# Selective scans: VectorE's C rows from SBUF through 128-fold DMA, and a fourth decay buffer

## The reference

```python
x_dbl = einsum('bld,ed->ble', x_conv, x_proj_w)      # splits into dt_in, B, C
delta = softplus(einsum('blr,dr->bld', dt_in, dt_proj_w) + dt_proj_b)
dA = exp(delta[:, :, None] * A)                      # the decay
h  = h * dA + (delta * u)[:, :, None] * B[:, None, :] # the scan over the tokens
y  = einsum('bdn,bn->bd', h, C)                      # sum over the states
```

## Time and profile before

| what | us |
|---|---|
| three runs: median (lowest to highest) | 3246.61 (3240.67 to 3251.88) |
| the profiled execution | 3240.62 |
| its span | 3238.9 |
| the stage's loop, first to last scan and product | 776.5 |
| busy over the span: TensorE / VectorE / ScalarE / GpSimd | 2954.5 / 2151.4 / 1625.0 / 1076.9 |

### The profile page before, as it was taken

How to read it: one execution, slowest core, us unless ns; L and a number is a source line. 1 busy time by engine, 2 the same in 40 slices (tenths; PEclk the granted TensorE clock), 3 DMA queues, 4 the chain that set the end, 5 groups by cost and what they waited for, 6 DMA issues and landing times. The chain is left out here.

```text
span 3238.9 us, 58361 instructions
## 1 busy us (share of the span) xinstructions
PE 2954.5 (91%) x22601; PEld 1697.9 (52%) x22601; DVE 2151.4 (66%) x4823; ACT 1625.0 (50%) x3321; POOL 1076.9 (33%) x504
## 2 busy tenths in 40 slices
PE   7888899999899999998977998898889889988998
PEld 3333344444799999743434544444454344564547
DVE  6776634545777777666568887777871559936991
ACT  3545542432433333426266776776753657725762
POOL 1111100000300000000078877777850209922990
PEclk8999999999655555699988999999899999999999
DMA  5343332022000000030442222222310101250224
GB/s 156 94 111 90 89 108 84 8 78 80 16 4 4 4 4 4 2 107 1 143 142 88 77 94 86 80 82 73 98 41 41 61 1 68 99 198 0 91 98 188
DMA packets 113492, 234.32 MB, mean 72 GB/s; under 512 B 13760, under 2 KB 50752, under 8 KB 104768
## 3 DMA queue, kind: packets, MB, share of 16 engines
q1 hardware_dynamic: 113216, 230.59, 21.9%
HBM read 185.71 MB, written 44.83 MB: 71 GB/s over the span
## 5 line engine op out<-in xcount | busy, mean ns | idle before, releaser
L2547 DVE TENSOR_TENSOR_SCAN s_hh<-psum,s_dbu 128x512 f32<-128x512 f32 x384 | 447.6, 1208 | 77.3 <-ACT psum L2159 76.1
L1272 PE MATMUL psum<-h_ring,h_parts 128*128 128x4 f16 x12264 | 478.0, 168 | 3.8 <-DVE h_ring L1414 3.5
L2417 POOL TENSOR_TENSOR s_dbu<-s_du,s_bb 128x1024 f32<-128x1024 f32 x191 | 446.7, 2360 | 67.1 <-DVE s_hh L2547 56.0
L1272 PEld LDWEIGHTS psum<-h_ring,h_parts 128*128 128x128 f16 x12264 | 429.8, 106 | 51.9 <-DVE h_ring L1414 4.2
L1334 ACT ACTIVATE h_now<-psum 128x16 f32<-128x16 f32 x1024 | 187.3, 183 | 326.8 <-PE psum L1272 322.3
L2159 ACT ACTIVATE psum<-s_delta,s_decay 128x512 f32<-128x512 f32 x384 | 256.6, 686 | 109.1 <-DVE s_hh L2547 107.0
L2051 PEld LDWEIGHTS psum<-w_c,s_term 128*128 128x128 f32 x1536 | 202.3, 151 | 136.7 <-issue 117.5
L911 DVE TENSOR_TENSOR f_hid<-f_gate,psum 128x512 f32<-128x512 f32 x184 | 126.5, 687 | 205.2 <-PE psum L837 198.2
L902 POOL MEMSET r_weights<- 128x512 f32 x4 | 2.1, 524 | 777.1 <-POOLq L1224 507.3
L1414 DVE TENSOR_SCALAR h_ring<-h_now 128x16 f16<-128x16 f32 x1024 | 183.8, 179 | 115.0 <-ACT h_now L1334 11.7
L898 ACT ACTIVATE f_gate<-psum 128x512 f32<-128x512 f32 x184 | 109.6, 597 | 281.9 <-PE psum L833 281.8
(11 more groups left out here) (543 smaller groups left out, 6047.5 us busy)
## 6 DMA issues: line engine op xcount, KB each, us to landing
s_bb<-s_wide SPq DMA_DIRECT2D x192, 256.0 KB, 3.5
x_spill<-x_flip SPq DMA_DIRECT2D x28, 1024.0 KB, 3.8
f_share<-f_wide SPq DMA_DIRECT2D x208, 128.0 KB, 3.0
s_cc<-s_wide SPq DMA_DIRECT2D x60, 256.0 KB, 3.4
a_ks<-a_spread SPq DMA_DIRECT2D x96, 128.0 KB, 3.3
a_qs<-a_spread SPq DMA_DIRECT2D x96, 128.0 KB, 3.9
x_spare<-x_spill SPq DMA_DIRECT2D x4, 2048.0 KB, 7.7
x_raw<-x_spill SPq DMA_DIRECT2D x4, 2048.0 KB, 7.5
```

The source lines that it names most:

```text
L1272: mm = nc.tensor.matmul(here[:, cols], parts[:, part, GROUP * grp + p, :], ring[:, (i - 1) % RING, grp, cut, cols], start=False, stop=True ...
L2417: nc.gpsimd.tensor_tensor(dbu[:, s % D_RING], du[:, t % 2], both(bb[:, s % B_RING, :]), ALU.mult).then_inc(dbu_ready, 1)
L2547: nc.vector.tensor_tensor_scan(hh[:, s % 4, half, :], DECAYS[i % 3], dbu[:, s % D_RING, half, :], 0.0, ALU.mult, ALU.add).then_inc(scan_do ...
```

## The change

VectorE's C products no longer read from PSUM. SP fetches the C row of every step to all partitions: `cc` gets a ring of 6, indexed by s, and the C row of step s is issued behind the B row of step s + 4. Each waits for the product with C of six steps before, whichever engine made it. With that `pick_c`, its table, GpSimd's cast, the bf16 parts, the small matmuls and four of ScalarE's five copies a turn go. Bank 3 now only carries the second half of the rates. The decay ring gets a fourth buffer in SBUF (`fourth`), so that instruction i waits for scan i - 4, and every fourth scan reads its decay from SBUF.

```diff
-    DECAYS = (bank[1], bank[4], bank[5])
+    DECAYS = (bank[1], bank[4], bank[5], fourth[:, :])
-    B_RING, C_RING = 6, 3
+    B_RING, C_RING, C_LATER = 6, 6, 4
+    DECAY_RING = 4
...
         def c_there(eng, s):
-            eng.wait_ge(c_in[pool_steps(s) % C_RING], 16 * (pool_steps(s) // C_RING + 1))
+            eng.wait_ge(c_in[s % C_RING], 16 * (s // C_RING + 1))
+        def c_used(eng, s):
+            if by_vector(s):
+                eng.wait_ge(term_vector, vector_steps(s) + 1)
+            else:
+                eng.wait_ge(term_pool, pool_steps(s) + 1)
...
                     open_pre(("rate", t))
-                    pe.wait_ge(dt_kept, t + 1)
+                    parts_there(pe, t)
-                    pe.wait_ge(term_vector, vector_steps(s))
-                    nc.tensor.matmul(PICK_C, w[f"dtw{r}"][:, P:2 * P], dt[0:rank, :], start=True, stop=True).then_inc(rate_ready, 1)
+                    pe.wait_ge(delta_done, t)
+                    nc.tensor.matmul(RATE, w[f"dtw{r}"][:, P:2 * P], small[0:rank, :], start=True, stop=True).then_inc(rate_ready, 1)
...
-                def pick_c(s):
-                    t, n = divmod(s, N)
-                    if n == 1 and t:
-                        pe.wait_ge(pre_free, pre_at[("parts", t)] + 1)
-                    if vector_steps(s):
-                        pe.wait_ge(term_vector, vector_steps(s))
-                    if t + 1 < TURNS and n == rate_slot(t) // 2 + 1:
-                        pe.wait_ge(delta_done, t + 2)
-                    nc.tensor.matmul(PICK_C, g.pick_c[0:96, n, :], bc[:, t % 2, :],
-                                     start=True, stop=True).then_inc(c_spread, 1)
...
-                    if i >= 3:
-                        act.wait_ge(scan_done, i - 2)
+                    if i >= DECAY_RING:
+                        act.wait_ge(scan_done, i - DECAY_RING + 1)
...
                     act.wait_ge(pre_ready, pre_at[("parts", t)] + 1)
-                    if t >= 2:
-                        act.wait_ge(c_spread, vector_steps((t - 1) * N))
                     act.wait_ge(rows_stored, 16 * t)
-                    nc.scalar.copy(rows, bc_rows(t)).then_inc(rows_kept, 1)
-                    nc.scalar.copy(bc[0:32, t % 2, :], bc_rows(t)).then_inc(hi_kept, 1)
-                    nc.scalar.copy(dt[0:rank, :], PRE[0:rank, :]).then_inc(dt_kept, 1)
+                    nc.scalar.copy(small[0:width, :], PRE[0:width, :]).then_inc(pre_free, 1)
...
-                pool.wait_ge(g.picks_loaded, 16)
-                nc.gpsimd.tensor_copy(g.pick_c.rearrange("p n m -> p (n m)"), picks_there).then_inc(tables_cast, 1)
...
-                    nc.vector.tensor_tensor_scan(hh[:, s % 4, half, :], DECAYS[i % 3], dbu[:, s % D_RING, half, :], 0.0,
+                    nc.vector.tensor_tensor_scan(hh[:, s % 4, half, :], DECAYS[i % DECAY_RING], dbu[:, s % D_RING, half, :], 0.0,
                                                  ALU.mult, ALU.add).then_inc(scan_done, 1)
...
-                    dve.wait_ge(c_spread, vector_steps(s) + 1)
+                    c_there(dve, s)
                     if s >= 4:
                         dve.wait_ge(y_added, 2 * (s - 4) + 2)
-                    nc.vector.tensor_tensor(term[:, s % 4], hh[:, s % 4], both(PICK_C), ALU.mult).then_inc(term_vector, 1)
+                    nc.vector.tensor_tensor(term[:, s % 4], hh[:, s % 4], both(cc[:, s % C_RING, :]), ALU.mult).then_inc(term_vector, 1)
...
-                sp.dma_start(picks_there, g.pick_table).then_inc(g.picks_loaded, 16)
-                for s in range(STEPS):
-                    if not by_vector(s):
-                        k = pool_steps(s)
-                        if k >= C_RING:
-                            sp.wait_ge(term_pool, k - C_RING + 1)
-                        sp.dma_start(cc[:, k % C_RING, :], wide[t, N + n:N + n + 1, :].broadcast_to([P, CHUNK])
-                                     ).then_inc(c_in[k % C_RING], 16)
+                for s in range(STEPS + C_LATER):
+                    if s >= C_LATER:
+                        c = s - C_LATER
+                        t, n = divmod(c, N)
+                        if c >= C_RING:
+                            c_used(sp, c - C_RING)
+                        sp.dma_start(cc[:, c % C_RING, :], wide[t, N + n:N + n + 1, :].broadcast_to([P, CHUNK])).then_inc(c_in[c % C_RING], 16)
```

## The result

The changed kernel takes 3344.86 us (median; 3341.97 to 3348.62) against 3243.64 before (3236.79 to 3251.88): a ratio of 1.0309, 95% interval 1.0292 to 1.0327. It is 101 us slower. The forecast was 3400, with a range of 3268 to 3455 for all cases and of 3345 to 3455 for its own. The profiled execution has a span of 3341.6 us against 3238.9.

The account below looks back on a forecast made before the run. Scan, product and decay pace the old stage; afterwards GpSimd and two-SBUF-input VectorE work exclude each other: 621.8 + 159.2 + 111.9 = 892.9, plus 40 idle, 933 us. 3240.6 + 156.5 - 2 = 3395, median 3400, range 3268 to 3455.

Parts of the forecast that it names:

- Parts 1 and 2: Scan stage: 132 C products (159.2 us) and 96 scans with SBUF decays (111.9 us) newly need exclusive turns with GpSimd.
- The taps: Second layer's taps, a VectorE instruction with two SBUF inputs: 1209 ns alone, 5460 beside GpSimd; read as waiting two whole GpSimd instructions.
- the two scalings: Two 128x128 scalings: 280 ns before the stage, 1446 and 2384 beside GpSimd products; taken as further evidence of exclusion.
- The rival that only the products contend: Scan stage: C products wait for GpSimd, SBUF scans do not; 3289 us (3260 to 3330), chance 0.20.
- The sum: Scan stage: 892.9 us of exclusive claims plus 40 idle gives 933 against 776.5, so +156.5 us.
- part 5: Handing over turns between VectorE and GpSimd in the scan stage: 0 us, bounds -23 to +25.
- Part 4: Scan stage: time neither engine uses the exclusive path, 20 for GpSimd's waits, 10 at the end, 10 for slow places.
- Part 6: VectorE's removed waits, 23.4 us for spreading and at most 53 for decays, are worth nothing beside a full path.
- Part 7: SP's queue: issuing 192 C rows instead of 60 costs 0, at most 20 us in all.
- Part 8: Start of the stage: the 1 MB table, GpSimd's cast and two copies fall away, -2 us (-3 to 0).
- What would show it: Scan stage signs: locked products and scans near 2 us, decay waits under 30, no spread waits, GpSimd products at 2.36.
- The clock: TensorE's granted clock (mean 0.91) drops and it bounds the stage below 0.59: 3460 us and up, chance 0.06.

Follow-up runs that it names:

- e5: Kernel before with a 128x64 VectorE product, both inputs in SBUF, added in front of each of its 132 C products: 3294.95 us.
- e6: Kernel before with the same 132 added 128x64 VectorE products, but the second input from PSUM: 3251.52 us.
- e2: Kernel before with only the fourth decay buffer in SBUF added, C still read from PSUM: 3277.85 us.
- e4: Changed kernel with all 192 C products on VectorE and none on GpSimd: 3329.65 us.
- e7: Changed kernel with the fourth decay buffer in PSUM (bank 3) and both halves of the rates through bank 0, one behind the other: 3260.03 us.
- e3: Kernel before with the other 132 C rows also fetched by DMA, into a tile that nobody reads: 3244.83 us.
- e1: Changed kernel with the fourth decay buffer taken out again, so all scans read their decay from PSUM: 3253.04 us.
- e10: Kernel before with 4 of VectorE's 11 C products a turn reading C from SBUF, the other 7 still from the spreading matmul: 3256.80 us.

## Why the prediction was right

**Direction and mechanism** were right: slower, the two-input instructions wait for GpSimd, and those with one input in PSUM don't (e5 against e6, and L2495 against itself). Parts 1 and 2 of the forecast stand, the second with its choice: scans do contend, 2097 against 1202 ns. The taps of the earlier trace rows, one instruction of the old trace, were enough for this. Two readings beside them were loose. The taps asked 0.3 us after a product had started, so they waited for the rest of one product and for the next. And the two scalings of the earlier trace rows read one tensor and one value a partition; they don't show that a second input counts, but that the rule reaches further (last section). The rival that only the products contend falls with the scans' 2097 ns.

**The sum** gave a loop of 933 us; it took 875 (778 before). The loop was forecast to grow by 156.5 and grew by 97. The measured 3344.86 lies in the whole range, but at the very bottom of the forecast's own, 3345 to 3455, not near its 3400. The term that was mis-sized is part 5, the handing over. I took 0 with bounds of -23 and +25; the 58 us that the sum is too high lie far outside them. Where the engines alternate, five GpSimd products take 16.34 us, 3.27 each, with one VectorE instruction between two:

```profile
2074.43 16.34 POOL L2369 TENSOR_TENSOR s_dbu<-s_du,s_bb 128x1024 f32<-128x1024 f32 x5
```

I had 2.36 + 1.20 = 3.56. Each pair overlaps by some 0.29 us in the records; if all 228 did, it would be 66 us, and 933 would come to 867. The measured 875 asks for 0.25 a pair. The old trace had the sign (0.12 us before GpSimd's recorded end). Against it I set the 0.13 us of the earlier trace rows, which is the start of a product that waits for a scan by semaphore; where the product behind is already waiting for its turn, I take it that this does not arise. That the rest is only 8 us is partly luck: not all 228 meet a product, and e2 and e4 show that waits from the order of the work come on top of the sum.

**Part 4**, the idle time of the path: GpSimd waited 15.0 us for a delta, 6.3 for reciprocals and 35.2 for scans in the new loop, 56.5 in all. I counted 40 and named other causes. VectorE can use the path in these waits, so they are an upper bound, and 40 is neither confirmed nor refuted.

**Part 6**, waits that end beside a full path are worth nothing: right as a whole (118.5 us of idle VectorE time turned into waits inside instructions). Its figure of up to 53 us for a fourth buffer is too high: 19 us in e2, 2 in e7.

**Part 7**, the DMA and SP's queue at 0: right (e3, and no VectorE product of the changed kernel waited for a row: idle 0.0 before L2503). **Part 8**, -2 at the start: the loop now begins 25.1 us after the first layer's taps (1615.6 to 1640.7) against 25.3 (1611.2 to 1636.5), so nothing.

**What would show it**: durations, decay waits (23.3, under 30) and spread waits came as named. Wrong was that GpSimd's products stay at 2.36: their means are 3.0 and 3.3 us, since GpSimd's wait for a turn also lies inside its duration. In 16 us there are 7.0 scans in the mean (384 x 16 / 875), at the edge of the forecast 6 to 7; the single stretches of 16 us hold 4 to 9 by their starts.

**The clock** fell from 0.91 to 0.85 in the loop, less than the rival wanted. TensorE stood still for 220 of the 875 us, and for 123 of the 778 before. Its share in the loss was not measured by itself. That e1, at 0.90 and with the same TensorE work, is near the old time speaks for a consequence of the longer loop, but doesn't prove it.

## What to carry to other kernels

Before moving an operand from PSUM to SBUF, count for each VectorE instruction how many of its inputs then lie in SBUF and how busy GpSimd is beside it. With two, the fp32 products and scans here waited for GpSimd's product to end and the other way round, down to a size of 128x64; with one in PSUM none did. The price was small for products that GpSimd's rest had room for (8.5 us for 132) and grew at once when it hadn't (101 us with 96 scans more). Room is not enough for scans, on which the decays wait: 96 of them alone cost 33 us. In a profile such waits are no idle time; look for one line of code with two means by operand, and for a maximum that lies one instruction of the other engine above the minimum.

## What the runs showed that was not expected

The turn does not always change at the end of an instruction. In the changed kernel no product waited longer than for one GpSimd instruction (3403 ns at most). In e10 one waited for four, and two more of its 48 took 7599 and 3982 ns. GpSimd, then VectorE, in order of time:

```profile
1932.25 2.38 POOL L2425 TENSOR_TENSOR s_du<-s_delta,s_u 128x1024 f32<-128x1024 f32 x1
1934.57 6.96 POOL L2434 TENSOR_TENSOR s_dbu<-s_du,s_bb 128x1024 f32<-128x1024 f32 x3
...
1932.64 9.97 DVE L2575 TENSOR_TENSOR s_term<-s_hh,s_cc 128x1024 f32<-128x1024 f32 x1
```

GpSimd's four instructions follow each other at 2.32 us, undisturbed, until its ring of products is full; only then VectorE runs. The taps of the earlier trace rows met the same. That one instruction took 5460 ns in the old kernel, 7607 in e3, 4580 in e6, and 1194 in the changed kernel, where it got its turn at once. How late in GpSimd's instruction VectorE asks does not decide it alone. It was passed over having asked 0.4 us after a start here, and again having asked 1.8 us after one (the 3982 ns of e10). In between, at 0.46 us, it got its turn at the next boundary (in e1, at 2102.57, for 2.99 us, beside products from 2102.11). What decides is open. A two-input instruction on VectorE can therefore cost several GpSimd instructions in a row.

Two inputs in SBUF are not the only case. Behind the taps VectorE turns the sign of a 128x32 table, with one input in SBUF and a constant. The first line is the kernel before, where GpSimd rests at that moment, the second the changed kernel, beside five GpSimd products (from 1702.47, for 16.57 us):

```profile
L2526 DVE TENSOR_SCALAR w_l2b<-w_l2b x1: 171/171/171, 1696.5 to 1696.5; 128x32 f32<-128x32 f32 x1
L2474 DVE TENSOR_SCALAR w_l2b<-w_l2b x1: 2317/2317/2317, 1706.9 to 1706.9; 128x32 f32<-128x32 f32 x1
```

In e1, e2 and e5 it took 2331, 2320 and 2317 ns. So a scaling with a single input in SBUF waits too, and counting inputs does not find it. No run varied it by itself.
